# V' copied out of PSUM in full-width rows, and laid out by DMAs within SBUF

## The chip, the cores and the metric

One NeuronCore of a Trainium2 chip runs the kernel. TensorE (PE) multiplies and transposes, VectorE (DVE) and ScalarE (ACT) read PSUM and work element by element, GpSimd (POOL) works on SBUF, and SyncE (SP) issues the DMAs. The metric is the device time of one execution in microseconds (us); lower is better.

## The reference

Cross-attention and a quantized feed-forward network (FFN), for 128 sequences of 64 tokens with 128 features, in fp32. The attention has 16 heads of 64; the mask is causal. The FFN's weights are ternary and its activations are rounded to 8 bits.

```python
x = x + attention(layernorm(x), ctx, ctx, Wq, Wk, Wv, Wo, bo, mask)   # softmax(q k^T / 8) v, 16 heads of 64
x = x + ffn(layernorm(x), w_gate, w_up, w_down)
# bitlinear(a, w) = act_quant(a) @ weight_quant(w)^T
# ffn(a) = bitlinear(silu(bitlinear(a, w_gate)) * bitlinear(a, w_up), w_down)
```

## The kernel before

**Tiling.** Two sequences make a pair of 128 tokens, one per partition. There are 64 pairs, in 16 groups of four. The projections are folded: K' = ctx (Wk Wq^T / 8) for each head, so that the scores are layernorm(x) times K', and V' = ctx (Wv Wo) for each head, so that the product of the probabilities with V' is the attention's output, summed over the heads. K' and V' need the accuracy of fp32 and are made of three matmuls each (high x high, high x low, low x high parts).

**Slots.** The work runs in 64 slots, one per pair, and three more that drain the pipeline. In slot s, TensorE computes the scores of pair s, the product of pair s - 1 (L492 to L496), and transposes and FFN matmuls of pairs s - 1 to s - 3. Between these stand four units of V' of pair s (`v_quarter`, v0 to v3, L381) and four of K' of the next group (`k_quarter`, k0 to k3, L400), each of three matmuls of 512 columns into a PSUM bank. The order by hand is: scores; in a group's first slot v0; transposes, gate and up matmuls, in the other slots v0; transposes, k0, down matmul, v1, k1, product, v2, k2, k3, v3; and after v3 of a group's fourth slot the transposes of context and x of the group after next. The last group has no K' units in its slots. Each engine runs its own list in this order and waits on semaphores; nothing else sets the order.

**Banks.** V' units go to ps_s (v1, v2) and ps_kv (v0, v3), K' units to ps_kv (k0, k3) and ps_s (k1, k2). A bank can be written again once ScalarE has copied it: K' quarter 2 waits on `k_evac` for the copy of quarter 1 (L408), and the scores, which use both ps_s banks, wait for the copies of v2 and k2, in a group's first slot also for that of k3.

**V' and its layout.** A unit of V' is made for 128 context tokens, with columns for 4 of the 8 head pairs and 128 features. u // 2 says which head of a pair it is (h2), u % 2 which half of the head pairs. The product contracts over the 64 tokens of both heads of a pair together, so that it wants `vp[h2 * 64 + token, b, head pair, feature]`, with sequence b of the pair in the free dimension. PSUM has sequence b in the partitions. `take_v` (L576) therefore makes two copies a unit, one for each sequence, each of 64 partitions x 512, from partitions b * 64 on to partitions h2 * 64 on. That is eight such copies a slot, each with a count on `v_evac`. The product waits for eight a slot.

**ScalarE's order in a slot** (L594 to L625): xq_t, hid_t, probabilities' first half, tanh, v0, probabilities' second half, k0, v1, the exponential of pair s (which waits on POOL's subtraction of the row maximum), k1, v2, k2, k3, v3, and in a group's fourth slot context and x of a later group.

**SP's order**: after the setup's loads, for each group, the loads of x and context of the group after next, the load of the residual's x for the next group, and the store of the group before.

Of the kernel before, what the change touches and what calls it, by code (L numbers as in the profile page):

```python
# [40 lines left out]
def build(nc, x, ctx, mask, wq, wk, wv, wo, bo, w_gate, w_up, w_down, ident, causal, chooser, out):  # L41
# [19 lines left out]
    with ExitStack() as es:  # L61
# [41 lines left out]
        x1 = [sb(f"x1_{i}", [P, GP, D]) for i in range(2)]  # L103

        vp = [sb(f"vp{i}", [P, 2, HP, D]) for i in range(2)]
        prob = [sb(f"prob{i}", [P, H, S]) for i in range(2)]
        prob_t = sb("prob_t", [P, HP, P])
        row_max = [sb(f"row_max{i}", [P, H]) for i in range(2)]
# [43 lines left out]
        x_loaded = [sem(f"x_loaded{i}") for i in range(2)]  # L152
        xres_loaded = [sem(f"xres_loaded{i}") for i in range(2)]
        stored = [sem(f"stored{i}") for i in range(2)]

        const_set, absum_done, mean_ready, mean_done, tern_step = (sem(n) for n in (
            "const_set", "absum_done", "mean_ready", "mean_done", "tern_step"))
# [50 lines left out]
        @block.sync  # L208
        def _(sp):
            sp.dma_start(mask_u8.rearrange("b (p j) -> b p j", j=S),  # L210
                         mask.rearrange("(p b) j -> b p j", b=2)).then_inc(mask_in, 16)
            sp.dma_start(causal_sb[:], causal).then_inc(small_in, 16)
            sp.dma_start(choose_f[:], chooser).then_inc(small_in, 16)
            sp.dma_start(id_sb[:], ident).then_inc(id_in, 16)
            for w, src in enumerate((wk, wq, wv)):
                sp.dma_start(w_raw[w], src).then_inc(wqkv_in[w], 16)
            sp.dma_start(x_in[0][:], x_g[0]).then_inc(x_loaded[0], 16)
            sp.dma_start(ctx_in[0][:], ctx_g[0]).then_inc(ctx_loaded[0], 16)
            for w, t in enumerate((w_gate, w_up)):
                sp.dma_start(f_raw[:, w, :].rearrange("p (a d) -> p a d", d=D),  # L220
                             t.rearrange("(a p) d -> p a d", p=P)).then_inc(ffn_in, 16)
            sp.dma_start(f_raw[:, 2, :], w_down).then_inc(ffn_in, 16)
            sp.dma_start(wo_sb, wo.rearrange("(a p) e -> p a e", p=P)).then_inc(wo_in, 16)
            sp.dma_start(bo_sb[:], bo.rearrange("(o d) -> o d", o=1).broadcast_to([P, D])).then_inc(bo_in, 16)
            sp.dma_start(x_in[1][:], x_g[1]).then_inc(x_loaded[1], 16)
            sp.dma_start(ctx_in[1][:], ctx_g[1]).then_inc(ctx_loaded[1], 16)
            sp.dma_start(x_res[0][:], x_g[0]).then_inc(xres_loaded[0], 16)

            def group(it, par):

                g = 2 * it + par
                dyn = lambda v, k: v[g + k] if isinstance(it, int) else v[bass.ds(g + k, 1)].rearrange(
                    "o p q d -> (o p) q d")
                if group_ahead(it, par * GP, 2):
                    sp.wait_ge(xn_ready, GP * g + GP)
                    sp.dma_start(x_in[par][:], dyn(x_g, 2)).then_inc(x_loaded[par], 16)
                    sp.wait_ge(ctxt_ready, g + 1)
                    sp.dma_start(ctx_in[par][:], dyn(ctx_g, 2)).then_inc(ctx_loaded[par], 16)
                if group_ahead(it, par * GP, 1):
                    if not isinstance(it, int) or g:  # L240
                        sp.wait_ge(x1_done, GP * g)
                    sp.dma_start(x_res[1 - par][:], dyn(x_g, 1)).then_inc(xres_loaded[1 - par], 16)
                if not isinstance(it, int) or g:
                    sp.wait_ge(x2_done, GP * g)
                    sp.dma_start(dyn(out_g, -1), x1[1 - par][:]).then_inc(stored[1 - par], 16)

            for it in range(BODIES):
                for par in range(2):
                    group(it, par)

            sp.wait_ge(x2_done, PAIRS - 1)
            sp.dma_start(out_g[GROUPS - 1][:, 0:GP - 1, :], x1[1][:, 0:GP - 1, :]).then_inc(stored[1], 16)
            sp.wait_ge(x2_done, PAIRS)
            sp.dma_start(out_g[GROUPS - 1][:, GP - 1, :], x1[1][:, GP - 1, :]).then_inc(stored[1], 16)
            sp.wait_ge(stored[0], 16 * BODIES)
            sp.wait_ge(stored[1], 16 * (BODIES + 1))
# [3 lines left out]
        def _(pe):  # L260
# [116 lines left out]
            def slot(it, c):  # L377
# [3 lines left out]
                def v_quarter(u):  # L381

                    v_dst = banks[v_bank(it, c, u)]
                    if live(it, c):
                        if first(it, c):
                            pe.wait_ge(n_lo_done, u + 1)
                        if u == 0 and live(it, c, 1):
                            pe.wait_ge(v_evac, 8 * s)
                        elif u == 1:
                            pe.wait_ge(biased, s + 1)  # L390
                        elif u and group_ahead(it, c, 1):
                            pe.wait_ge(v_evac, 8 * s + (4, 2)[u == 3])
                        h2, half = u // 2, u % 2
                        hi, lo = (w[:, h2, 4 * half:4 * half + 4, :].rearrange("p a e -> p (a e)") for w in (n_hi, n_lo))
                        cols = slice(q * P, q * P + P)
                        mm(v_dst, ct_hi[par][:, cols], hi, start=True, stop=False)  # L396
                        mm(v_dst, ct_hi[par][:, cols], lo, start=False, stop=False)  # L397
                        mm(v_dst, ct_lo[par][:, cols], hi, start=False, stop=True).then_inc(v_ready, 1)  # L398
# [12 lines left out]
                if live(it, c):  # L411
# [4 lines left out]
                    if first(it, c):  # L416
                        pe.wait_ge(mean_done, 1)
                    if live(it, c, 1):
                        pe.wait_ge(v_evac, 8 * s - 2)
                        if not isinstance(it, int) or group_ahead(it, c - 1, 1):  # L420
                            pe.wait_ge(k_evac, 16 + 4 * s - 1)
                    for half in range(2):
# [63 lines left out]
                if live(it, c, 1):  # L486

                    pe.wait_ge(pt_evac, 2 * s)
                    pe.wait_ge(v_evac, 8 * s)
                    if live(it, c, 3):  # L490
                        pe.wait_ge(x2_done, s - 2)
                    for a in range(HP):  # L492
                        for b in range(2):
                            t = mm(ps_a[b * S:(b + 1) * S, 0:D], prob_t[:, a, b * S:(b + 1) * S],  # L494
                                   vp[(c - 1) % 2][:, b, a, :], start=(a == 0), stop=(a == HP - 1))
                    t.then_inc(attn_ready, 1)  # L496
# [16 lines left out]
        def _(act):  # L513
# [58 lines left out]
            def slot(it, c):  # L572
# [3 lines left out]
                def take_v(u):  # L576
                    if live(it, c):

                        h2, half = u // 2, u % 2
                        act.wait_ge(v_ready, 4 * s + u + 1)  # L580
                        for b in range(2):
                            copy(flat(vp[c % 2][h2 * S:(h2 + 1) * S, b, 4 * half:4 * half + 4, :]),
                                 banks[v_bank(it, c, u)][b * S:(b + 1) * S, :]).then_inc(v_evac, 1)

                def take_k_quarter(u):
                    if live(it, c) and group_ahead(it, c, 1):
# [328 lines left out]
```

## Time and profile before

| | us |
|---|---|
| median of 3 timed runs | 815.12 |
| lowest, highest | 815.04, 815.55 |
| the profiled execution | 815.8 |
| its span on the core | 814.0 |
| TensorE busy in it | 783.2 (96%) |
| ScalarE busy | 678.6 (83%) |
| VectorE busy | 677.9 (83%) |
| POOL busy | 406.9 (50%) |
| DMA traffic | 20.84 MB, 26 GB/s on average |

The profile records one execution by engine; times in its rows are microseconds from the start of the span, unless ns is said. "Busy" adds up the engine's instructions. Matmuls are pipelined and their ends are modelled, so a busy TensorE is not one at its peak. The chain is followed back from the last instruction: at each step to what released it, or to the instruction before it on its engine.

### The profile page before, as it was taken

The page shows a single profiled execution, that of the slowest core. Times are in us where ns is not written, and L with a number is a line of the kernel's source. Part 1 is how long each engine was busy: PE and PEld are TensorE (multiplying, and loading weights), DVE is VectorE, ACT ScalarE, POOL GpSimd, SP SyncE. Part 2 cuts the span into 40 slices and gives each one's busy share as a digit, 9 for nine tenths or more (in the row PEclk, how much of TensorE's full clock was granted, in tenths as well). Part 3 has the DMA queues.
Part 4 walks back from the last instruction along what each step waited for, and adds up shares of the span by engine and source line. Part 5 has one row for each costly group of instructions (what it writes and reads, how often), then busy time and mean ns, then how long its engine had stood idle before and what let it go on. Part 6 is the DMA issues. An engine that isn't in the chain of part 4 may idle for free.

```text
span 814.0 us, 15482 instructions
## 1 busy us (share of the span) xinstructions
PE 783.2 (96%) x5487; PEld 543.7 (67%) x5550; DVE 677.9 (83%) x1845; ACT 678.6 (83%) x1202; POOL 406.9 (50%) x404
## 2 busy tenths in 40 slices
PE   7899999999999999999999999999999999999983
PEld 5657667666766766666676676676676667667652
DVE  7749888888888888888888888888888888878894
ACT  4688888888888888988888888888888888888872
POOL 1234545455455555555555545555455554544551
PEclk9999999999999999999999999999999999999997
DMA  7200010000101001010100101010010100000000
GB/s 219 61 1 1 15 39 16 22 18 14 41 13 40 5 17 33 14 41 14 39 1 14 41 14 40 14 40 2 13 41 14 40 14 15 0 14 14 2 14 14
DMA packets 37123, 20.84 MB, mean 26 GB/s; under 512 B 1460, under 2 KB 36534, under 8 KB 37046
## 3 DMA queue, kind: packets, MB, share of 16 engines
q1 hardware_dynamic: 37046, 19.84, 8.5%
q8 instruction: 45, 0.74, 0.4%
q14 instruction: 32, 0.26, 0.1%
HBM read 15.64 MB, written 4.19 MB: 24 GB/s over the span
## 4 chain that ended last, share of the span: by engine, by line
PE 91%; DVE 4%; ACT 2%; issue 2%; POOL 1%; DMA 0%; POOLq 0%; DVEq 0%
PE ps_s L425 14%; PE ps_a L494 14%; PE ps_s L396 5%; PE ps_s L316 4%; PE ps_kv L396 4%; PE ps_kv L397 3%; PE ps_kv L316 3%; PE ps_kv L317 3%; PE ps_s L318 3%; PE ps_s L398 3%; PE ps_s L397 3%; PE ps_b L453 3%; PE ps_s L317 3%; PE ps_kv L398 3%; PE ps_kv L318 3%; PE ps_a L453 3%
## 5 line engine op out<-in xcount | busy, mean ns | idle before, releaser
L866 POOL TENSOR_TENSOR prob<-prob,row_max 128x1024 f32<-128x1024 f32 x64 | 121.9, 1905 | 179.6 <-DVE row_max L741 179.6
L514 ACT ACTIVATE vp<-ps_s 64x512 f32<-64x512 f32 x256 | 151.2, 591 | 33.2 <-PE ps_s L398 28.9
L884 POOL TENSOR_TENSOR prob<-prob,row_rec 128x512 f32<-128x512 f32 x128 | 130.7, 1042 | 56.5 <-DVE row_rec L816 56.5
L514 ACT ACTIVATE vp<-ps_kv 64x512 f32<-64x512 f32 x256 | 151.5, 592 | 5.3
L876 POOL TENSOR_TENSOR hid_b<-hid_q,neg_round 128x512 bf16<-128x512 f32 x64 | 66.5, 1039 | 124.3 <-DVE hid_q L785 124.3
L494 PE MATMUL ps_a<-vp,prob_t 128*64 128x128 f32 x2048 | 125.9, 276 | 1.3 <-DVE x L763 1.2
L494 PEld LDWEIGHTS ps_a<-vp,prob_t 128*64 128x64 f32 x2048 | 110.6, 137 | 24.3 <-issue 16.3
L425 PE MATMUL ps_s<-kp,xn_t 128*64 128x512 f32 x512 | 124.0, 605 | 2.9 <-ACT vp L514 1.9
L738 DVE TENSOR_TENSOR prob<-ps_s,bias_sb 128x1024 f32<-128x1024 f32 x64 | 78.4, 1225 | 51.8 <-PE ps_s L425 51.7
L843 POOL TENSOR_TENSOR rs<-ve,neg_half 128x1 f32<-128x1 f32 x128 | 70.2, 548 | 42.0 <-DVE ve L663 25.0
L514 ACT ACTIVATE kp<-ps_s 128x512 f32<-128x512 f32 x130 | 77.8, 598 | 11.8 <-PE ps_s L284 8.0
L741 DVE TENSOR_REDUCE row_max<-prob 128x16 f32<-128x1024 f32 x64 | 78.1, 1220 | 2.2
L814 DVE TENSOR_REDUCE row_sum<-prob 128x16 f32<-128x1024 f32 x64 | 77.4, 1210 | 0.0
L514 ACT ACTIVATE kp<-ps_kv 128x512 f32<-128x512 f32 x122 | 72.3, 593 | 0.6 <-PE ps_kv L284 0.5
L425 PEld LDWEIGHTS ps_s<-kp,xn_t 128*64 128x64 f32 x512 | 31.0, 136 | 60.4 <-issue 55.3
L514 ACT ACTIVATE xq_t<-ps_u 128x128 bf16<-128x128 f32 x64 | 17.8, 278 | 62.7 <-PE ps_u L438 62.7
L570 ACT ACTIVATE prob<-prob 128x1024 f32<-128x1024 f32 x64 | 66.9, 1045 | 0.0
L396 PE MATMUL ps_s<-n_hi,ct_hi 128*128 128x512 f32 x128 | 62.5, 489 | 0.7 <-ACT vp L514 0.7
L396 PE MATMUL ps_kv<-n_hi,ct_hi 128*128 128x512 f32 x128 | 61.4, 480 | 0.0
L316 PE MATMUL ps_kv<-ct_hi,m_hi 128*128 128x512 f32 x120 | 52.5, 438 | 1.0 <-ACT wd_t L514 1.0
L754 DVE SCALAR_TENSOR_TENSOR gated<-tanh_sb,ps_g 128x512 f32<-128x512 f32 x64 | 43.9, 687 | 10.2 <-ACT tanh_sb L606 8.8
L316 PE MATMUL ps_s<-ct_hi,m_hi 128*128 128x512 f32 x128 | 52.0, 406 | 0.3
(175 smaller groups left out, 1734.8 us busy)
## 6 DMA issues: line engine op xcount, KB each, us to landing
x_in<-in_x SPq DMA_DIRECT2D x16, 256.0 KB, 3.9
ctx_in<-in_ctx SPq DMA_DIRECT2D x16, 256.0 KB, 4.4
x_res<-in_x SPq DMA_DIRECT2D x16, 256.0 KB, 2.8
out<-x SPq DMA_DIRECT2D x15, 256.0 KB, 2.5
kp<-in_L_xattn_Wk SPq DMA_DIRECT2D x1, 512.0 KB, 3.7
kp<-in_L_xattn_Wq SPq DMA_DIRECT2D x1, 512.0 KB, 4.6
kp<-in_L_xattn_Wv SPq DMA_DIRECT2D x1, 512.0 KB, 5.5
kp<-in_L_xattn_Wo SPq DMA_DIRECT2D x1, 512.0 KB, 6.1
```

The lines of the kernel that those rows point to most:

```text
L316: mm(dst, hi, ct_hi[par][:], start=True, stop=False)
L396: mm(v_dst, ct_hi[par][:, cols], hi, start=True, stop=False)
L425: t = mm(ps_s[b * S:(b + 1) * S, half * BANK:(half + 1) * BANK], xn_t[par][:, cols], kp[par][:, half * 8:half * 8 + 8, cols], start=True, ...
L494: t = mm(ps_a[b * S:(b + 1) * S, 0:D], prob_t[:, a, b * S:(b + 1) * S], vp[(c - 1) % 2][:, b, a, :], start=(a == 0), stop=(a == HP - 1))
L514: copy = lambda dst, src, **kw: nc.scalar.activation(dst, src, ACT.Copy, **kw)
L570: nc.scalar.activation(prob[c % 2][:], prob[c % 2][:], ACT.Exp).then_inc(exp_done, 1)
L738: v.tensor_tensor(prob[c % 2][:], ps_s[:, :].rearrange("p (h j) -> p h j", j=S), pair_bias.broadcast_to([P, H, S]), ALU.add).then_inc(bias ...
L741: v.tensor_reduce(row_max[c % 2][:], prob[c % 2][:], AX, ALU.max).then_inc(max_done, 1)
L814: v.tensor_reduce(row_sum[:], prob[c % 2][:], AX, ALU.add).then_inc(sum_step, 1)
L843: p.tensor_tensor(dst[:], src[:], neg_half[:], ALU.pow).then_inc(done, 1)
L866: p.tensor_tensor(prob[c % 2][:], prob[c % 2][:], rows(row_max[c % 2]), ALU.subtract).then_inc(shifted, 1)
L884: p.tensor_tensor(prob[c % 2][:, heads, :], prob[c % 2][:, heads, :], rows(row_rec[c % 2])[:, heads, :], ALU.mult).then_inc(normed, 1)
```

## The change

`take_v` makes one copy a unit, of all 128 partitions, into a new tile `v_rows[h2]` that has the partitions of PSUM (token within sequence b). When both units of an h2 are copied, SP issues two DMAs, one for each sequence, that bring 64 partitions x 4096 bytes from `v_rows[h2]` to `vp`. That is four DMAs a slot. They count on `v_moved[h2]`, 32 a slot. The product waits on both of these and no longer on `v_evac`; ScalarE waits on `v_moved[h2]` of the slot before when it writes `v_rows[h2]` again; and SP waits for the product of the pair before the last (`attn_ready`) before it writes `vp`. `v_evac` counts 4 a slot, with the same meaning for the banks as before. SP's list is now written slot by slot: the group's loads and stores stand between the moves. The loads of x and context, for three groups ahead, come in the third slot, that of the residual in the second, the store in the fourth.

```diff
+        v_rows = [sb(f"v_rows{i}", [P, HP, D]) for i in range(2)]
...
+        v_moved = [sem(f"v_moved{i}") for i in range(2)]
...
+            def load_inputs(g):
+                par = g % 2
+                sp.wait_ge(xn_ready, GP * (g - 2) + GP)
+                sp.dma_start(x_in[par][:], x_g[g]).then_inc(x_loaded[par], 16)
+                sp.wait_ge(ctxt_ready, g - 1)
+                sp.dma_start(ctx_in[par][:], ctx_g[g]).then_inc(ctx_loaded[par], 16)
+
+            def slot(it, c):
+                s = BODY * it + c
+                g, q, par = 2 * it + c // GP, c % GP, c // GP % 2
+                if q == 3 and g > 0 and live(it, c):
+                    sp.wait_ge(x2_done, GP * g)
+                    sp.dma_start(out_g[g - 1], x1[1 - par][:]).then_inc(stored[1 - par], 16)
+                for h2 in range(2):
+                    if live(it, c):
+                        sp.wait_ge(v_evac, 4 * s + 2 * h2 + 2)
+                        if live(it, c, 2):
+                            sp.wait_ge(attn_ready, s - 1)
+                        for b in range(2):
+                            sp.dma_start(vp[c % 2][h2 * S:(h2 + 1) * S, b, :, :],
+                                         v_rows[h2][b * S:(b + 1) * S, :, :]).then_inc(v_moved[h2], 16)
+                if q == 1 and live(it, c) and group_ahead(it, c, 1):
+                    if g:
+                        sp.wait_ge(x1_done, GP * g)
+                    sp.dma_start(x_res[1 - par][:], x_g[g + 1]).then_inc(xres_loaded[1 - par], 16)
+                if q == 2 and live(it, c) and group_ahead(it, c, 3):
+                    load_inputs(g + 3)
+
+            load_inputs(2)
+            slots(slot, 0)
...
-                    pe.wait_ge(v_evac, 8 * s)
+                    pe.wait_ge(v_moved[0], 32 * s)
+                    pe.wait_ge(v_moved[1], 32 * s)
...
                         act.wait_ge(v_ready, 4 * s + u + 1)
-                        for b in range(2):
-                            copy(flat(vp[c % 2][h2 * S:(h2 + 1) * S, b, 4 * half:4 * half + 4, :]),
-                                 banks[v_bank(it, c, u)][b * S:(b + 1) * S, :]).then_inc(v_evac, 1)
+                        if live(it, c, 1):
+                            act.wait_ge(v_moved[h2], 32 * s)
+                        copy(flat(v_rows[h2][:, 4 * half:4 * half + 4, :]), banks[v_bank(it, c, u)]).then_inc(v_evac, 1)
```

The other changed waits follow the new count of `v_evac` (8 * s becomes 4 * s, and so on).

On ScalarE, from the tanh of a slot on, before: L514 is the copy, L570 the exponential, and x2 stands for two instructions of the same kind in a row.

```order
L606 ACTIVATE tanh_sb<-ps_g,g_half 128x512
L514 ACTIVATE vp<-ps_kv 64x512 x2
L514 ACTIVATE prob_t<-ps_b 128x512
L514 ACTIVATE kp<-ps_kv 128x512
L514 ACTIVATE vp<-ps_s 64x512 x2
L570 ACTIVATE prob<-prob 128x1024
L514 ACTIVATE kp<-ps_s 128x512
L514 ACTIVATE vp<-ps_s 64x512 x2
```

The same place on ScalarE now:

```order
L619 ACTIVATE tanh_sb<-ps_g,g_half 128x512
L527 ACTIVATE v_rows<-ps_kv 128x512
L527 ACTIVATE prob_t<-ps_b 128x512
L527 ACTIVATE kp<-ps_kv 128x512
L527 ACTIVATE v_rows<-ps_s 128x512
L583 ACTIVATE prob<-prob 128x1024
L527 ACTIVATE kp<-ps_s 128x512
L527 ACTIVATE v_rows<-ps_s 128x512
```

The order is the same; each pair of half-height copies is one of full height, so that two copies fewer stand ahead of the exponential and of the K' copy behind it.

On SP, the DMAs of some groups of the steady part, before: loads of x and context, load of the residual's x, store.

```order
L236 DMA x_in<-in_x 128x4x128 [waits xn_ready]
L238 DMA ctx_in<-in_ctx 128x4x128 [waits ctxt_ready]
L242 DMA x_res<-in_x 128x4x128 [waits x1_done]
L245 DMA out<-x_0 128x4x128 [waits x2_done]
L236 DMA x_in<-in_x 128x4x128 [waits xn_ready]
```

The same on SP now, from the second slot of a group to the store in the fourth:

```order
L251 DMA vp<-v_rows 64x1024 [waits attn_ready,v_evac]
L251 DMA vp<-v_rows 64x1024
L256 DMA x_res<-in_x 128x4x128 [waits x1_done]
L251 DMA vp<-v_rows 64x1024 [waits attn_ready,v_evac]
L251 DMA vp<-v_rows 64x1024
L251 DMA vp<-v_rows 64x1024 [waits attn_ready,v_evac]
L251 DMA vp<-v_rows 64x1024
L235 DMA x_in<-in_x 128x4x128 [waits xn_ready]
L237 DMA ctx_in<-in_ctx 128x4x128 [waits ctxt_ready]
L244 DMA out<-x_0 128x4x128 [waits x2_done]
```

Two moves follow each half's copies, and the loads and the store of a group have moved in among them.

On TensorE, the product (L494 before) and what stands around it:

```order
L318 MATMUL ps_s<-ct_hi,m_lo 128x512
L494 MATMUL ps_a<-vp,prob_t 64x128 [waits x2_done,v_evac,pt_evac]
L494 MATMUL ps_a<-vp,prob_t 64x128 x15
L396 MATMUL ps_s<-n_hi,ct_hi 128x512 [waits v_evac]
L397 MATMUL ps_s<-n_lo,ct_hi 128x512
L398 MATMUL ps_s<-n_hi,ct_lo 128x512
```

And now (L507 is the product):

```order
L330 MATMUL ps_s<-ct_hi,m_lo 128x512
L507 MATMUL ps_a<-vp,prob_t 64x128 [waits v_moved1,x2_done,v_moved0,pt_evac]
L507 MATMUL ps_a<-vp,prob_t 64x128 x15
L408 MATMUL ps_s<-n_hi,ct_hi 128x512 [waits v_evac]
L409 MATMUL ps_s<-n_lo,ct_hi 128x512
L410 MATMUL ps_s<-n_hi,ct_lo 128x512
```

Nothing has changed its place on TensorE; the product waits for the moves in place of the copies.

## Rows read from the trace of the kernel before

**Rows 1.** The page: busy time (share of the span) by engine, and the last chain.

```profile
PE 783.2 (96%) x5487; PEld 543.7 (67%) x5550; DVE 677.9 (83%) x1845; ACT 678.6 (83%) x1202; POOL 406.9 (50%) x404
...
PE 91%; DVE 4%; ACT 2%; issue 2%; POOL 1%; DMA 0%; POOLq 0%; DVEq 0%
```

**Rows 2.** Groups by line and shape: out<-in, shapes, count, busy us, mean ns, idle before.

```profile
L514 ACT ACTIVATE vp<-ps_kv 64x512 f32<-64x512 f32 x256 | 151.5, 592 | 5.3
...
L514 ACT ACTIVATE kp<-ps_s 128x512 f32<-128x512 f32 x130 | 77.8, 598 | 11.8 <-PE ps_s L284 8.0
```

**Rows 3.** Busy us by engine in two stretches; last: TensorE's clock, DMA share, GB/s.

```profile
400.00:500.00 100.00, 99.53 (x715) 69.29 (x722) 85.84 (x239) 86.62 (x155) 52.95 (x54) 1.00 0.11 30
...
760.00:780.00 20.00, 18.41 (x148) 12.33 (x147) 19.02 (x50) 16.70 (x30) 11.06 (x10) 1.00 0.04 13
```

**Rows 4.** The chain in a group's first slot: start us, us, engine, tile, line.

```profile
427.63 0.02 issue
427.66 0.50 PE ps_s L316
```

**Rows 5.** Waits between 60 and 740 us: in total, times, longest.

```profile
PEld ps_s L316 <- ACT kp L514: 6.6, 15, 0.5
```

**Rows 6.** Timeline of the same slot, ScalarE and POOL: start us, us, instruction.

```profile
425.94 1.04 ACT L570 ACTIVATE prob<-prob 128x1024 f32<-128x1024 f32 x1
427.01 0.60 ACT L514 ACTIVATE kp<-ps_s 128x512 f32<-128x512 f32 x1
...
422.43 1.91 POOL L866 TENSOR_TENSOR prob<-prob,row_max 128x1024 f32<-128x1024 f32 x1 [2.40 <-DVE row_max L741]
```

**Rows 7.** The chain in slots 0 and 1.

```profile
44.34 0.60 ACT vp L514
...
47.89 0.23 PE ps_kv L398
...
53.82 1.90 PE ps_a L494 x32
```

**Rows 8.** Timeline of slot 60 on TensorE and VectorE: start us, us, instruction, idle before.

```profile
752.87 1.94 PE L425 MATMUL ps_s<-kp,xn_t 128*64 128x512 f32 x8 [0.30 <-ACT kp L514]
...
758.33 1.97 PE L494 MATMUL ps_a<-vp,prob_t 128*64 128x128 f32 x32
...
760.63 0.28 DVE L801 TENSOR_TENSOR x<-ps_a,x_res 128x128 f32<-128x128 f32 x1
```

**Rows 9.** The chain in two steady slots.

```profile
404.48 0.23 PE ps_kv L318
...
405.18 0.23 PE ps_kv L398
...
412.17 1.90 PE ps_a L494 x32
...
417.08 0.44 PE ps_b L274 x4
```

**Rows 10.** The page's DMA issues: count, KB each, median us from issue to landing.

```profile
ctx_in<-in_ctx SPq DMA_DIRECT2D x16, 256.0 KB, 4.4
x_res<-in_x SPq DMA_DIRECT2D x16, 256.0 KB, 2.8
...
kp<-in_L_xattn_Wk SPq DMA_DIRECT2D x1, 512.0 KB, 3.7
kp<-in_L_xattn_Wq SPq DMA_DIRECT2D x1, 512.0 KB, 4.6
```

**Rows 11.** Timeline of SP's issues, at the start and in one group: start us, us.

```profile
2.27 0.43 SPq L216 DMA_DIRECT2D kp<-in_L_xattn_Wk  x1
2.74 0.43 SPq L216 DMA_DIRECT2D kp<-in_L_xattn_Wq  x1
...
400.09 0.51 SPq L236 DMA_DIRECT2D x_in<-in_x  x1
400.64 0.56 SPq L238 DMA_DIRECT2D ctx_in<-in_ctx  x1
```

More of the change, by code:

```diff
@@ L227, in _ @@
             sp.dma_start(x_res[0][:], x_g[0]).then_inc(xres_loaded[0], 16)
[L229 to L240, printed above, removed]
-                        sp.wait_ge(x1_done, GP * g)
[L242 to L245, printed above, removed]
@@ L247, in _ @@
-            for it in range(BODIES):
-                for par in range(2):
-                    group(it, par)
+            def load_inputs(g):
[20 more added lines that the diff above has]
+                    if g:
+                        sp.wait_ge(x1_done, GP * g)
+                    sp.dma_start(x_res[1 - par][:], x_g[g + 1]).then_inc(xres_loaded[1 - par], 16)
+                if q == 2 and live(it, c) and group_ahead(it, c, 3):
+                    load_inputs(g + 3)
@@ L387, in v_quarter @@
                         if u == 0 and live(it, c, 1):
-                            pe.wait_ge(v_evac, 8 * s)
+                            pe.wait_ge(v_evac, 4 * s)
                         elif u == 1:
@@ L391, in v_quarter @@
                         elif u and group_ahead(it, c, 1):
-                            pe.wait_ge(v_evac, 8 * s + (4, 2)[u == 3])
+                            pe.wait_ge(v_evac, 4 * s + (2, 1)[u == 3])
                         h2, half = u // 2, u % 2
@@ L418, in slot @@
                     if live(it, c, 1):
-                        pe.wait_ge(v_evac, 8 * s - 2)
+                        pe.wait_ge(v_evac, 4 * s - 1)
                         if not isinstance(it, int) or group_ahead(it, c - 1, 1):
@@ L488, in slot @@
                     pe.wait_ge(pt_evac, 2 * s)
-                    pe.wait_ge(v_evac, 8 * s)
+                    pe.wait_ge(v_moved[0], 32 * s)
+                    pe.wait_ge(v_moved[1], 32 * s)
                     if live(it, c, 3):
```

## The prediction

> **What bounds the kernel now.** I read the page's busy times first: TensorE is busy for 783.2 of 814.0 us, VectorE and ScalarE for 678 each, and the chain of work that ended last lies on TensorE for 91% and on ScalarE for 2% [rows 1]. So ScalarE's 151.5 us of copies of V' out of ps_kv, and as much again out of ps_s [rows 2], are no price by themselves. The question is where TensorE waits for ScalarE. The table by stretch says how much room there is: in 400 to 500 us TensorE is busy for 99.53 of 100 us at the full granted clock [rows 3]. But a busy row hides short waits, since matmuls are pipelined, so I read the chain in order of time and looked for pieces longer than their like. Between 50 and 750 us every kind of piece has one price wherever it stands (a matmul of 512 columns that follows its like 0.23 or 0.24 us, the product 1.90), with one exception: in the first slot of groups 1 to 14, the first matmul of K' quarter 2 takes 0.50 us after 0.02 of issue [rows 4]. The wait is for ScalarE: the weight loads of that line sat for 6.6 us in 15 times until a copy of K' ended [rows 5], which is 0.46 in each of these 14 slots and 0.18 in an early one that TensorE does not feel. In that slot ScalarE has also taken the next group's context and x out of PSUM, and is late from there on: v0, v1 (two copies each), the exponential from 425.94, then the K' copy that ends at 427.61 [rows 6].
>
> Two more places: at the start, the second of two copies of V' in a row stands in the chain with 0.60 us [rows 7]; and near the end the scores of slot 60 begin at 752.87 after 0.30 us of waiting for a copy of K' [rows 8]. From there VectorE takes over: from 760 to 780 us it is busy for 19.02 of 20, TensorE for 18.41 and ScalarE for 16.70 [rows 3]. TensorE's waits for ScalarE in slots 61 to 63 therefore cost nothing.
>
> **What is removed: four of eight copies a slot.** A copy of 64 partitions x 512 takes 592 ns; one of 128 x 512 out of the same kind of bank (a K' copy) 598 [rows 2]. The time goes by columns, so each pair becomes one of 0.59: ScalarE loses 4 x 0.59 = 2.4 us a slot, 151 us in all. On the path this gives:
> - First slots of groups 1 to 14. Since v0 and v1 take one copy each, ScalarE reaches the exponential 1.2 us earlier, at about 424.8 instead of 425.94; POOL's subtraction, its input, ends at 424.34 [rows 6], so the full 1.2 can be had up to 0.4. Then the copy of K' quarter 1 ends at about 426.4, and the weight load that wants it could begin 0.46 before 427.66, at 427.2. The piece falls from 0.02 + 0.50 to 0.23: 0.29 us each, **14 x 0.29 = 4.1 us**.
> - Start: one of two copies in the chain goes: **0.6 us**.
> - Slot 60: the copy ahead of the two K' copies is 0.6 shorter, so the 0.30 wait goes: **0.3 us**. VectorE's pace from there on stays.
> - All other slots: nothing. The chain is TensorE work there, and less work on ScalarE moves none of it.
>
> **What is added: the moves.** Four a slot, each 64 partitions x 4096 bytes = 256 KB, 64 MB in all, on SP's queue. Three things have to be seen.
>
> First, who waits. The product of pair s in slot s + 1 now waits for both halves. The half that counts is the second, since v3 is the last unit of slot s; the first half is issued half a slot earlier, with some 12 us to spare. ScalarE waits for a half before it writes v_rows again: v0 of the next slot for moves issued some 8 us earlier, and v2 for moves that the product ahead of it has waited for already; nothing there.
>
> Second, the budget. In a steady slot the last matmul of v3 ends at 405.18 + 0.23 = 405.41 and the product begins at 412.17 [rows 9], its first weight load some 0.1 earlier. v3's copy, no longer behind the pair of v2, runs from 405.43 to 406.03, so from SP's first issue to the landing of the second move there are **6.0 us**. In first slots of a group the transposes of context and x, two pieces of 0.44 [rows 9], lengthen it to 6.9. In slot 1, without the FFN's work, v3's last matmul ends at 47.89 + 0.23, its copy 0.61 later, and the product begins at 53.82: 5.0 with the 0.1 of the weight load [rows 7]. In slot 60 the scores, which follow v3, begin at 752.57 without the wait, and the product at 758.33 - 0.30; that makes 4.9, and 0.3 more since VectorE takes the product's result only at 760.63, 0.3 after its end [rows 8].
>
> Third, the landing. No row shows a DMA from SBUF to SBUF, nor one of 64 partitions. Lower bound: the 256 KB loads of x_res land 2.8 us after issue [rows 10]; with a second issued 0.43 later that is 3.2 us. Nearest in form are the weight loads at the start, with the same 4096 bytes a partition, 512 KB each: two issued at 2.27 and 2.74 us land after 3.7 and 4.6 [rows 10, 11], that is 1.37 us apart, and 3.7 - 1.37 = 2.3 us is fixed. At this full rate a 256 KB move drains in 0.69 and the second lands after 2.3 + 2 x 0.69 = 3.7. Half the partitions may carry no more than half the rate, and I take that: 2.3 + 2 x 1.37 = **5.1 us**. A pair of loads from DRAM, x_in and ctx_in, gives nearly this by another way: issued at 400.09 and 400.64, 0.55 + 4.4 = 4.95 [rows 10, 11]. Upper bound: reading and writing the same memory halve the rate again, 2.3 + 2 x 2.74 = 7.8 us. I take 5.1, since two different rows come close to it: under the budget of 6.0 by 0.9, so hidden; over that of slot 1 by about **0.2 us**, which I count as a loss; in slot 60 covered by VectorE's 0.3.
>
> The Trainium skill, in "SBUF — State Buffer", section "Door 1: The DMA port swizzle", has a rule that speaks against moves of this shape: partitions 0 to 63 (or 64 to 127) reach only 8 of 16 DMA ports, 196 GB/s measured at 1 MiB; and its section "Can I just issue two DMAs to hit both halves?" says that two such transfers run one after the other. By its figures two moves would take about 2 + 2 x 1.3 = 4.6 us, an estimate from that page; with full rate on its 16 ports it would be 3.2. Either is under 6.0 and leaves the sum as it is. No run here shows it yet.
>
> SP's queue: four issues of 0.43 [rows 11] are 1.7 us of a slot of some 12. The loads and the store of a group now stand between moves, at places where what they wait for was done a slot earlier; the x_in and ctx_in loads go behind the second half of the third slot, and the next move is half a slot away. Before this they were waited for nowhere; x_in is loaded one slot or more ahead of its first reader. Nothing.
>
> **Sum.** 4.1 + 0.6 + 0.3 - 0.2 = 4.8 us. The profiled execution took 815.8 us with a span of 814.0; the median of the timed runs is 815.12. I expect a span of about 809.2 and a median of 815.1 - 4.8 = **810.3 us**.
>
> **Rivals.**
> - *The moves land late.* The distance from v3's copy to the product becomes longer than the TensorE work between, and TensorE stands before the product in every slot. At the upper bound of 7.8: 44 steady slots x 1.8 + 14 first slots x 0.9 + 2.8 in slot 1 + 4 last ones x 2.6 = 105 us, less 5.0 gained: 915 us. The point from which it decides is low: 4.8 us lie in 44 x 0.11, so the kernel is slower from a landing at 6.1 us. For it: no row shows such a transfer. Against it: the DMA engines have a share of only 0.11 here [rows 3], and both near rows say 5. Chance 0.18.
> - *The 14 stalls stay*, because the exponential waits for POOL's subtraction or for something in front of it that I see only from outside. Then 0.6 + 0.3 - 0.2 = 0.7 is left: 814.4 us. Against it: 0.4 us of room at the exponential and 0.8 at the K' copy. Chance 0.09.
> - *The moves' traffic slows the engines a little*, or a few slots are late by a tenth. The moves drain for some 5.5 of 12 us; 0.08 us lost per slot takes all of the gain: 815 us. Against it: while the 512 KB of loads issued at 400.09 and 400.64 were under way, a matmul at 404.48 kept its 0.23 [rows 9, 11]. Chance 0.08.
>
> **How the numbers follow.** My forecast has 0.65, with 809 to 812 of its own. A measurement of this kernel can tell about 0.2%, 1.6 us. The second and third rival lie within that: 0.17. Faster 0.65, same 0.17, slower 0.18. The range reaches from 808.8 (slot 1 not late, and a little more at the end) over both middle cases and the mildest of the late ones, a landing at up to 6.1 or 6.2, to 818; what is left out is most of the first rival.
>
> **What would show it.** ScalarE about 527 us busy. In the chain, K' quarter 2's first matmul at 0.23 in all first slots. The product's matmuls preceded by no wait for a DMA except in slot 1. DMA share near 0.4 to 0.5 in the steady stretch, moves landing 3 to 4.5 us after their issue. What makes it wrong: waits for a DMA at the product in steady slots, so that more than 6.76 us lie between the end of v3 and the product (405.41 to 412.17 [rows 9]).

## The result and the profile after

| | before | after |
|---|---|---|
| median of 5 timed runs, us | 815.55 | 811.62 |
| lowest, highest | 815.04, 816.84 | 811.16, 812.50 |
| the profiled execution | 815.8 | 811.4 |
| its span | 814.0 | 809.6 |

The ratio is 0.9953 with an interval of 0.9938 to 0.9967: faster by half a percent, clear of the noise, by 3.9 us in the medians and 4.4 in the spans. The forecast was a gain of 4.8 us.

The page of the kernel after, its busy times, chain and DMA issues (to be held against [rows 1, 10]):

```profile
PE 783.0 (97%) x5550; PEld 544.5 (67%) x5550; DVE 678.4 (84%) x1845; ACT 532.9 (66%) x946; POOL 407.4 (50%) x404
...
PE 89%; DVE 6%; issue 1%; DMA 1%; ACT 1%; POOL 1%; POOLq 0%; SPq 0%; DVEq 0%
...
vp<-v_rows SPq DMA_DIRECT2D x256, 256.0 KB, 3.7
```

ScalarE is busy for 532.9 us in place of 678.6, and TensorE for the same 783: 146 us of work gone, 4 us of time. The copies, by line and shape, have half their count at the same price (592 ns before [rows 2]):

```profile
L527 ACT ACTIVATE v_rows<-ps_kv 128x512 f32<-128x512 f32 x128 | 76.7, 599 | 6.7
```

The stretch of [rows 3], 400 to 500 us, in the same columns:

```profile
400.00:500.00 100.00, 100.00 (x700) 68.58 (x699) 85.76 (x240) 67.36 (x120) 54.31 (x54) 1.00 0.45 109
```

TensorE has no idle time left in it (99.53 before), and the DMA engines have a share of 0.45 where they had 0.11. The chain in the same slot as [rows 4]; L328 is the line that was L316:

```profile
422.29 1.90 PE ps_a L507 x32
424.18 0.43 PE ps_s L408
424.62 0.23 PE ps_s L409
424.85 0.24 PE ps_s L410
425.09 0.23 PE ps_s L328
```

The piece of 0.50 with 0.02 of issue before it is now one of 0.23. The timeline of ScalarE and POOL shows why [rows 6]:

```profile
419.87 1.91 POOL L879 TENSOR_TENSOR prob<-prob,row_max 128x1024 f32<-128x1024 f32 x1 [2.41 <-DVE row_max L754]
...
421.63 0.60 ACT L527 ACTIVATE v_rows<-ps_s 128x512 f32<-128x512 f32 x1
422.12 1.05 ACT L583 ACTIVATE prob<-prob 128x1024 f32<-128x1024 f32 x1
423.07 0.59 ACT L527 ACTIVATE kp<-ps_s 128x512 f32<-128x512 f32 x1
```

The subtraction ends at 421.78, the exponential follows at 422.12, and the K' copy is done at 423.66, 1.4 us before the matmul at 425.09 that needs its bank. In the trace of before that copy ended at 427.61, for a matmul at 427.66.

**One product is late.** In the whole trace the product waits for a DMA once (0.4 us in all, 1 time, 0.4 the longest):

```profile
PE ps_a L507 <- DMA vp<-v_rows: 0.4, 1, 0.4
```

The chain there:

```profile
545.92 0.61 ACT v_rows L527
...
546.54 0.46 SPq L251
547.00 0.04 issue
547.04 5.73 DMA vp<-v_rows
552.78 0.25 issue
553.02 1.97 PE ps_a L507 x32
```

And SP's issues behind that move (start us, us):

```profile
547.69 0.62 SPq L235 DMA_DIRECT2D x_in<-in_x  x1
548.36 1.51 SPq L237 DMA_DIRECT2D ctx_in<-in_ctx  x1
549.91 1.15 SPq L244 DMA_DIRECT2D out<-x  x1
```

This second move landed 5.73 us after its issue. It is the slowest of the 256, whose minimum, median and maximum are:

```profile
DMA to landing us min/median/max: 2.9/3.7/5.7
```

The pair before it in the same place of its group, issued at 498.87, took 3.3 and 3.9, so its second landed some 4.4 us after the first issue. So the loads and the store behind it do not by themselves do this.

Another row of the trace goes with the long landings. Besides SP's transfers the DMA engines carry two queues that the profile calls `instruction`; by that name they bring the program's own instructions. While the late pair was under way, from 546.5 to 552.8 us, a packet of each ran (queue: packets, MB, share of the 16 engines):

```profile
q8 instruction: 1, 0.02, 0.9%
q14 instruction: 1, 0.01, 0.3%
```

From 498.8 to 503.4 us, with the pair that has the same loads behind it, there was none. And in slot 16 (237.1 to 242.6 us), where SP issues no load or store between this pair and the next, the second move landed 5.4 us after the first issue, with one such packet under way:

```profile
q8 instruction: 1, 0.02, 1.1%
```

Over the whole trace, no pair without an `instruction` packet in flight has its second landing later than 4.64 us after its first issue, and each of the four slowest pairs of the second half (slots 9, 16, 29 and 42, 5.4 to 6.2 us) has a q8 packet in flight. Three further traces that have one late product (ScalarE's rounding and the two with added matmuls, below) show the same, with 4.60 to 4.64 as the limit. Not every such packet goes with a long landing: some pairs with one under way land after 4.2 to 4.4. So the `instruction` packets are the first suspect; no experiment moved them, so this stays a coincidence in the rows and not a shown cause.

**The end.** In the last slot TensorE stands idle for long stretches, and then runs at a granted clock of 0.55 of 2.4 GHz on average (800 is near the end of the span; columns as in [rows 3]):

```profile
798.00:802.00 4.00, 2.28 (x11) 1.16 (x11) 1.85 (x6) 1.52 (x3) 0.00 (x0) 0.55 0.00 0
```

The kernel before does the same: its clock is 0.60 in 802 to 804 us and 0.50 from there on.

### The profile page after: what moved, and what is told of

Its sections match the earlier page's. It is cut to its first block, busy times and chain, and to the rows that moved or that the text cites. A ratio compares the mean times of both kernels' runs of the same rounds, so it can differ in the third digit from the quotient of the medians.

```text
span 809.6 us, 15983 instructions
## 1 busy us (share of the span) xinstructions
PE 783.0 (97%) x5550; PEld 544.5 (67%) x5550; DVE 678.4 (84%) x1845; ACT 532.9 (66%) x946; POOL 407.4 (50%) x404
## 4 chain that ended last, share of the span: by engine, by line
PE 89%; DVE 6%; issue 1%; DMA 1%; ACT 1%; POOL 1%; POOLq 0%; SPq 0%; DVEq 0%
PE ps_s L437 14%; PE ps_a L507 14%; PE ps_s L408 5%; PE ps_kv L408 4%; PE ps_s L330 3%; PE ps_kv L328 3%; PE ps_s L328 3%; PE ps_kv L329 3%; PE ps_s L329 3%; PE ps_kv L409 3%; PE ps_s L410 3%; PE ps_s L409 3%; PE ps_kv L410 3%; PE ps_kv L330 3%; PE ps_b L465 3%; PE ps_a L465 3%
## 5 line engine op out<-in xcount | busy, mean ns | idle before, releaser
L527 ACT ACTIVATE v_rows<-ps_s 128x512 f32<-128x512 f32 x128 | 76.7, 599 | 106.8 <-PE ps_s L410 106.5
L507 PE MATMUL ps_a<-vp,prob_t 128*64 128x128 f32 x2048 | 125.9, 276 | 1.6 <-DVE x L776 1.2
L507 PEld LDWEIGHTS ps_a<-vp,prob_t 128*64 128x64 f32 x2048 | 110.6, 137 | 24.7 <-issue 21.8
L527 ACT ACTIVATE v_rows<-ps_kv 128x512 f32<-128x512 f32 x128 | 76.7, 599 | 6.7
L408 PE MATMUL ps_s<-n_hi,ct_hi 128*128 128x512 f32 x128 | 62.5, 489 | 0.1
L408 PE MATMUL ps_kv<-n_hi,ct_hi 128*128 128x512 f32 x128 | 61.4, 480 | 0.0
L328 PE MATMUL ps_kv<-ct_hi,m_hi 128*128 128x512 f32 x120 | 52.6, 438 | 1.0 <-ACT wd_t L527 1.0
L409 PE MATMUL ps_kv<-n_lo,ct_hi 128*128 128x512 f32 x128 | 51.0, 398 | 0.0
```

The costliest lines, as they stand in the source:

```text
L328: mm(dst, hi, ct_hi[par][:], start=True, stop=False)
L527: copy = lambda dst, src, **kw: nc.scalar.activation(dst, src, ACT.Copy, **kw)
```

## The experiments

All are held against runs of the kernel before on the same chip in the same session; its median was 815.85 for the half-height copies without counts, the other order, and the one or two more moves; 815.83 for the moves over 128 partitions and ScalarE's rounding alone; 815.54 for the others.

### Where the gain comes from

**Half-height copies again, with the moves kept.** An edit of the kernel after:

```diff
-copy(flat(v_rows[h2][:, 4 * half:4 * half + 4, :]), banks[v_bank(it, c, u)]).then_inc(v_evac, 1)
+for b in range(2):
+    rows = slice(b * S, b * S + S)
+    t = copy(flat(v_rows[h2][rows, 4 * half:4 * half + 4, :]), banks[v_bank(it, c, u)][rows, :])
+t.then_inc(v_evac, 1)
```

> The changed kernel with its four moves a slot, but each unit of V' copied in two half-height copies again, now into v_rows. If the gain comes from the shorter work of ScalarE alone, ScalarE's busy time is back at about 680 us, the 14 stalls before K' quarter 2 stand again in first slots (0.50 instead of 0.23 us), the second copy stands in the chain of slot 0, and the time is that of before, about 815.5 us. If the moves, or the new order of SP's loads, brought it, the time stays at 811.6.

Measured: 818.34 us (817.57 to 819.71), ratio 1.0035, interval 1.0022 to 1.0047. All of the gain is gone, so it came from the copies; and 2.5 us more are lost than the kernel before has. The first slots lose 0.35 us each in place of 0.25 (from one down matmul to the next 12.02 us, where it is 11.67 in the kernel after and 11.92 in the one before); that is 1.4. The rest is at four products that wait for a move (1.4 us in all) and in the last slots. The last of the four (product, start us, us, idle before):

```profile
791.07 1.97 PE L507 MATMUL ps_a<-vp,prob_t 128*64 128x128 f32 x32 [0.58 <-DMA vp<-v_rows]
```

With eight copies a slot the last one of v3 ends at least one copy (0.6) later, and the budget of the moves shrinks by that. The profiled execution is the slowest of the five (819.71), and 0.66 us of its longer span lie ahead of slot 0, where the kernels do the same work: the first scores begin at 34.02 us there. In the other traces, of both kernels and of the other experiments, they begin between 32.32 and 33.77 us, so a few tenths of any difference between two spans are of this kind.

**The same with a count on each copy**, as the kernel before has it, so that SP, TensorE and the copies wait on counts of 8 a slot. It asks whether the 0.10 more per first slot comes from the pair's first copy having no count of its own.

```diff
-sp.wait_ge(v_evac, 4 * s + 2 * h2 + 2)
+sp.wait_ge(v_evac, 8 * s + 4 * h2 + 4)
...
-copy(flat(v_rows[h2][:, 4 * half:4 * half + 4, :]), banks[v_bank(it, c, u)]).then_inc(v_evac, 1)
+for b in range(2):
+    rows = slice(b * S, b * S + S)
+    copy(flat(v_rows[h2][rows, 4 * half:4 * half + 4, :]),
+         banks[v_bank(it, c, u)][rows, :]).then_inc(v_evac, 1)
```

> The changed kernel with half-height copies again, as in the first experiment, but each copy counts for itself, as in the kernel before, and not the second for both. The first came out 2.8 us over the kernel before where I expected nothing: 1.4 of it were stalls before K' quarter 2 of 0.35 instead of 0.25 us. If that tenth comes from the missing count between two copies and not from the moves, it goes: about 816.9 us, with stalls of 0.25. If the moves cause it, they stay at 0.35 and the time at 818.3. The rest, products of the last slots that wait for a move, stays by either.

Measured: 818.55 us (818.26 to 819.64), ratio 1.0039, interval 1.0025 to 1.0052. The missing count is not the cause: first slots take 12.07, a stall of 0.40. By the expectation that points to the moves, but how they would do it is not seen in the chain of such a slot:

```profile
426.18 0.59 ACT v_rows L527
426.77 0.03 issue
426.80 1.06 ACT prob L583
427.86 0.02 issue
427.88 0.61 ACT kp L527
428.49 0.04 issue
428.53 0.50 PE ps_s L328
```

Here the exponential begins 0.03 after the end of the copy before it, while in the kernel before it began 0.09 before that end (copy pair until 426.03, exponential at 425.94). Why these instructions overlap less is open: the copies differ in their target and in ScalarE's wait for the last moves, and no run separated the two. In the last slots the chain is now a ring: copies, SP's issue, the move, the product, copies. Two of its moves, the first two rows with the product behind each:

```profile
776.06 3.73 DMA vp<-v_rows
...
780.04 1.97 PE ps_a L507 x32
...
785.91 4.08 DMA vp<-v_rows
...
790.24 1.97 PE ps_a L507 x32
```

**The kernel before with another order and no DMA.** If the first slots' stall is all that the copies cost, then ScalarE can have it back by making the K' copy ahead of the exponential in those slots:

```diff
+k_first = q == 0 and s > 0
+if k_first:
+    take_k_quarter(1)
 if live(it, c) and not first(it, c):
     exponential(s, c)
-take_k_quarter(1)
+if not k_first:
+    take_k_quarter(1)
```

> The kernel before, without any move, with one thing exchanged on ScalarE: in the first slot of groups 1 to 14 the copy of K' quarter 1 stands ahead of the exponential. If the stall of TensorE before quarter 2 is all that the change gains in the steady part, these 14 stalls of 0.25 us go and the time is 815.5 - 3.6 = about 812 us, with ScalarE as busy as before. If the stall was only a mark in the records and the gain has another source, it stays at 815.5.

Measured: 811.72 us (811.41 to 812.55), ratio 0.9954, interval 0.9942 to 0.9967. That is the median of the change, with ScalarE busy for 678.2 us and not one move. First slots take 11.67, so the stall itself is worth 3.55 us over the 14 of them. That the medians agree to 0.1 us is partly luck. In the spans this order gains 4.1: the 3.55, and 0.8 ahead of slot 0, where it changes nothing (scores at 32.56 us, at 33.36 before), less some tenths at the end. The start and slot 60, which the change shortens by 0.9, are as long here as before. In the timeline of ScalarE the K' copy of that slot now stands ahead of the exponential, and TensorE's piece is one of 0.23:

```profile
423.46 0.60 ACT L514 ACTIVATE kp<-ps_s 128x512 f32<-128x512 f32 x1
423.95 1.05 ACT L570 ACTIVATE prob<-prob 128x1024 f32<-128x1024 f32 x1
```

### How much room the moves have

**One more move a slot** of 256 KB from v_rows into a spare tile, ahead of the second half's two and counted with them:

```diff
+if h2 == 1:
+    for n in range(1):
+        sp.dma_start(v_spare[n][S:2 * S, :, :], v_rows[1][n * S:(n + 1) * S, :, :]).then_inc(v_moved[1], 16)
 for b in range(2):
     sp.dma_start(vp[c % 2][h2 * S:(h2 + 1) * S, b, :, :],
...
-pe.wait_ge(v_moved[1], 32 * s)
+pe.wait_ge(v_moved[1], 48 * s)
```

> The changed kernel with one more move of 256 KB, to a spare tile, ahead of the two of the second half in each slot. In the changed kernel the second move lands some 4.4 us after the first issue, 1.1 after the other. With three the last lands after about 5.5. If the budget is 6.0 us in steady slots, they stay at 11.67; slot 1 (budget 5.0) and the last four (4.9 to 5.2) lose 1 to 2 us together: 812 to 814 us. If the margin is smaller than I think, by x us, it is 44 x more.

Measured: 817.97 us (816.36 to 820.25), ratio 1.0029, interval 1.0018 to 1.0041. In most steady slots nothing is lost (slots of 11.67 as before): the last of three moves lands 5.5 to 5.7 us after the first issue, just inside the budget. But ten products are late, and the waits of the whole trace are:

```profile
PE ps_a L511 <- DMA vp<-v_rows: 7.5, 10, 2.0
```

Six of them stand where the budget is small: slot 1 with 0.63, and the last five products of all. The other four (0.18 to 0.95 us) are single ones in the steady part. The last of all:

```profile
798.89 2.92 PE L511 MATMUL ps_a<-vp,prob_t 128*64 128x128 f32 x32 [2.04 <-DMA vp<-v_rows]
```

The expectation priced the last slots far too low.

**Two more moves a slot**, the same edit with `range(2)` and 64 for 48.

> The same with two more moves. The last lands after about 6.6 us, which is over the budget of 6.0 by 0.6 in 44 steady slots (26 us), under that of 6.9 in 14 first slots, over by 1.6 in slot 1 and by about 1.4 in each of the last four: 811.6 + 26 + 1.6 + 5.6 = about 845 us, with waits for a DMA before the product in the steady slots. If the budget is right but late moves are absorbed elsewhere, it is under 820.

Measured: 885.85 us (883.87 to 886.37), ratio 1.0856, interval 1.0841 to 1.0871. The waits of the whole trace, and one steady slot, first the product and then its chain from the first issue on:

```profile
PE ps_a L511 <- DMA vp<-v_rows: 67.1, 51, 2.7
```
```profile
419.61 1.97 PE L511 MATMUL ps_a<-vp,prob_t 128*64 128x128 f32 x32 [1.09 <-DMA vp<-v_rows]
```
```profile
412.43 0.46 SPq L253
...
414.25 5.02 DMA vp<-v_rows
419.27 0.34 issue
```

The product in the slot behind a group's first (at 406.81) waits for nothing, the other three of that group for 1.0 to 1.1 each; elsewhere single ones wait for up to 2.7. The last of four moves lands 6.84 us after the first issue (412.43 to 419.27), and the product begins 0.34 later. Without the wait it would have begun at 418.52, so what the landing may take is about 5.8 us and not 6.0. A first slot, which has 0.9 us more, just about holds 6.84. The expectation took 6.6 and 6.0, a wait of 0.6 where 1.0 to 1.1 came; that, the last slots and the single late ones are what it was short by. The first rival of the prediction was right in its mechanism, and its price is steep: two moves too many turn a gain of 4 us into a loss of 70.

**The same bytes over 128 partitions.** Each move takes all partitions and half of the columns:

```diff
-sp.dma_start(vp[c % 2][h2 * S:(h2 + 1) * S, b, :, :],
-             v_rows[h2][b * S:(b + 1) * S, :, :]).then_inc(v_moved[h2], 16)
+heads = slice(4 * b, 4 * b + 4)
+sp.dma_start(vp[c % 2][:, h2, heads, :], v_rows[h2][:, heads, :]).then_inc(v_moved[h2], 16)
```

> The changed kernel with moves of the same 256 KB, the same number and the same places in SP's list, but each over 128 partitions x 2048 bytes instead of 64 x 4096. It leaves the layout out: V' stays in the partitions it has in PSUM, so the output is another. If 64 partitions halve the rate, the second move of a pair lands earlier than 4.4 us after the first issue, by about 0.9: 3.5. If a transfer within SBUF has its rate whatever the partitions, it is 4.4 again. The time is 811.6 by either, since both are under the budget; the late single move of the profile (5.7 us) may be gone, 0.4 us less.

Measured: 811.31 us (810.51 to 812.22), ratio 0.9944, interval 0.9930 to 0.9957. The time hardly differs from that of the kernel after; the moves do:

```profile
vp<-v_rows SPq DMA_DIRECT2D x256, 256.0 KB, 2.5
```
```profile
400.00:500.00 100.00, 100.00 (x701) 68.61 (x700) 85.66 (x240) 67.35 (x120) 54.21 (x54) 1.00 0.31 109
```

They land 2.5 us after their issue where those of 64 partitions took 3.7, and the DMA engines are busy for 0.31 in place of 0.45, for the same 109 GB/s. The second of a pair lands 3.0 us after the first issue, where 3.5 was expected. No product waits for a move in this trace. The Trainium skill says in "SBUF — State Buffer", section "Door 1: The DMA port swizzle", that a transfer of partitions 0 to 63 or 64 to 127 reaches half of the ports; these two rows agree. The bytes per partition were halved together with it, and no run separates the two.

**The second half in four pieces of 128 KB**, two of them issued after v2:

```diff
-for h2 in range(2):
+for h2, heads, done in ((0, slice(0, 8), 2), (1, slice(0, 4), 3), (1, slice(4, 8), 4)):
...
-        sp.wait_ge(v_evac, 4 * s + 2 * h2 + 2)
+        sp.wait_ge(v_evac, 4 * s + done)
```

> The changed kernel with the second half's two moves cut in two by columns: 128 KB each, the first two issued already when v2 is copied, the last two after v3. If drain time is what stands between v3's copy and the landing, the last lands some 3.6 us after the issue that follows v3, instead of 4.4, and the one late product of the profile is gone: 811.2 us, the same within what can be told. If two more issues a slot (some 1 us of SP) or twice the number of moves get in the way, it is over 812.

Measured: 811.39 us (810.57 to 812.71), ratio 0.9950, interval 0.9936 to 0.9964. The 128 KB moves land after 2.3 us, the last of them 2.9 us after the issue that follows v3 (3.6 was expected), and no product waits for one:

```profile
vp<-v_rows SPq DMA_DIRECT2D x256, 128.0 KB, 2.3
```

The span is 808.8, against 809.6 with the one late product. In the medians, 811.39 and 811.62, the difference is too small to be told.

### The end of the kernel

**ScalarE takes a step of VectorE's in slots 60 to 63.** From slot 60 on VectorE sets the pace [rows 3], and ScalarE now has time. It makes the rounding of the hidden activations (hid_q, 0.5 us of VectorE a slot) there:

```diff
+if act_rounds(s):
+    act.wait_ge(h_step, H_STEPS * (s - 2) + 6)
+    copy(hid_q[:], hid[:], scale=qs3[:], bias=ROUND).then_inc(hq_ready, 1)
...
-v.tensor_scalar(hid_q[:], hid[:], qs3[:], ROUND, ALU.mult, ALU.add).then_inc(hq_ready, 1)
+if not act_rounds(s):
+    v.tensor_scalar(hid_q[:], hid[:], qs3[:], ROUND, ALU.mult, ALU.add).then_inc(hq_ready, 1)
```

> The changed kernel, with the rounding of the hidden layer (0.49 us on VectorE) done by ScalarE in slots 60 to 63, where it has the time now. If VectorE alone sets the pace of the last four slots (9.65 us), each becomes some 0.45 us shorter: about 809.9 us. If ScalarE's or TensorE's chain is close behind, little of it is seen: 811 or more.

Measured: 811.16 us (810.95 to 812.14), ratio 0.9946, interval 0.9932 to 0.9959. The slots become 9.59, 9.47 and 9.46 us long, from 9.78, 9.64 and 9.63: 0.17 to 0.19 each and not 0.45, since VectorE, with less to do, now waits for the product:

```profile
775.08 0.29 DVE L825 TENSOR_TENSOR x<-ps_a,x_res 128x128 f32<-128x128 f32 x1 [0.27 <-PE ps_a L510]
```

And the next slot takes 10.21 in place of 9.22, which gives it all back; the one behind it is shorter again, 8.24 in place of 8.83, so that 0.14 us are left from the down matmul of slot 61 to the last. The windows show what the long slot goes with:

```profile
786.00:788.00 2.00, 0.00 (x0) 0.00 (x0) 1.86 (x7) 0.60 (x1) 1.55 (x3) 1.00 0.36 104
788.00:790.00 2.00, 1.56 (x10) 1.47 (x11) 0.48 (x3) 0.88 (x2) 1.22 (x2) 0.51 0.90 229
```

After more than 2 us without a matmul TensorE comes back at a granted clock of 0.51, the level of 1.2 GHz, and a row of four transposes takes 0.87 us where it takes 0.44 at 2.4 GHz:

```profile
789.32 0.87 PE ps_a L468 x4
```

**Matmuls that nobody reads, in the last three slots.** They keep TensorE at work while it waits, alone and with the edit before. 8, 14 and 22 matmuls of 512 columns are added:

```diff
+keep_busy(s, (8, 14, 0)[s - PAIRS] if s >= PAIRS else 0)
...
+keep_busy(s, 22 if s == PAIRS + 2 else 0)
...
+def keep_busy(s, n):
+    if n:
+        pe.wait_ge(v_evac, 4 * PAIRS)
+    for _ in range(n):
+        mm(ps_s[:, 0:BANK], ct_hi[1][:, 0:P], n_hi[:, 0, 0:4, :].rearrange("p a e -> p (a e)"),
+           start=True, stop=True)
```

> The changed kernel with the same added matmuls after slot 63 and nothing else. In its profile the clock fell only after slot 64: the pieces of TensorE from 798 us on would be shorter by 0.15 + 0.22 + 0.2 + 0.2 = 0.8 us: 810.8. By the rival, 811.6 or more.

Measured alone: 810.15 us (810.03 to 811.20), ratio 0.9934, interval 0.9921 to 0.9948.

> The sixth experiment (ScalarE rounds in slots 60 to 63) with added matmuls on TensorE in its idle times after slot 63 (8, 14 and 22 of 512 columns, into a bank that nobody reads). There the granted clock fell to about half before slot 64's transposes, and what four slots had gained (0.5 us) was given back. If the clock of the tail is what it costs, the pieces there are as short as elsewhere (0.22 instead of 0.44 us for four transposes) and some 1.6 us go: 809.5 us. If the added matmuls only stand in the way, or the clock falls all the same, 811 or more.

Measured with ScalarE's rounding: **809.73 us** (809.00 to 810.69), ratio 0.9930, interval 0.9917 to 0.9942. It is the fastest median of all kernels here. The same windows in this kernel, and the one near the end:

```profile
788.00:790.00 2.00, 2.00 (x18) 1.47 (x16) 0.18 (x1) 1.35 (x4) 0.92 (x1) 1.00 0.75 197
...
798.00:802.00 4.00, 4.00 (x20) 2.98 (x21) 2.76 (x7) 1.07 (x2) 0.00 (x0) 1.00 0.16 49
```

The clock is 1.00 in both. The tail's slots are 9.46, 9.05 and 8.40 us long where the edit before had 9.46, 10.21 and 8.24. Against the kernel after, from the down matmul of slot 61 to the last (752.92 to 806.52 us there), the added matmuls alone save 0.43 us in the trace, while the medians differ by 1.5. The profiled execution of the added matmuls alone is its slowest (811.20, the others 810.03 to 810.62), its first scores begin 0.44 us later than in the kernel after, and it has the same late product, so the traces compare a slow one with a fast one. How much of the 1.5 is the clock is open; with ScalarE's rounding, the same stretch is 0.99 shorter with the added matmuls than without them. The intervals of these kernels and of the kernel after overlap, so that the order among them is less sure than that each beats the kernel before.

## Why the prediction was right, and where it was off

The forecast was 810.3 us, 4.8 less than the kernel before; 811.62 came, 3.9 less in the medians and 4.4 in the spans. Point by point, in the spans:

- **The first slots** were to give 14 x 0.29 = 4.1. From one product to the next the slot went from 11.92 to 11.66 or 11.67, 3.55 over the 14. The mechanism was right, and the half-height copies (back to a stall) and the other order (no stall without a move) both show it. The term was mis-sized by 0.03 to 0.04 each: the chain's pieces of 0.02 and 0.50 were held against one of 0.23, but the pieces around it give some of that back. The distance between two products would have been the better row.
- **The start** gave the 0.6 expected: TensorE's chain there has no copy in it (44.18 0.09 issue, then L408 at 44.27), where [rows 7] had one of 0.60, and from the scores of slot 0 to those of slot 1 it is 14.08 us in place of 14.70. **Slot 60** gave 0.3. Behind it VectorE's pace was to stay; between the products of slots 61 and 62 it is 9.63 us for 9.76.
- **Slot 1** was to be late by 0.2 and was not. The term behind it was the landing: 5.1 us from SP's first issue to the second landing was taken, 4.4 came. That 64 partitions drain more slowly was right (3.7 us to land, against 2.5 over 128), but the landings of a pair lie only 1.1 us apart for 256 KB, while 1.37 was taken, from loads of twice the bytes [rows 10, 11]. Two of these leave some 2.2 fixed where 2.3 was taken. What failed was the step 2.3 + 2 x 1.37, which let half the partitions halve the rate of a 512 KB load from DRAM. The estimate from the Trainium skill's page "SBUF — State Buffer", 4.6, was closer.
- **The budget** of 6.0 left 0.1 between landing and product for the first weight load; the chain has 0.25 there (552.78), and 0.34 with four moves. It is nearer 5.8. The 4.9 for slot 60 is 4.8 by the prediction's own way, since the weight load's 0.1 was not taken off. Neither changed the sum.
- **The one late product** at 553.02, 0.4 us, was not in the sum. The step that failed was "Nothing" for what else is on the DMA engines: the prediction looked at what moves wait for in SP's list, and took one landing for all. Six of the 128 pairs landed more than 5.3 us after their first issue, and each of them had an `instruction` packet in flight. Loads behind the moves cost less: the second half's pairs land after 4.45 us at the median in the slots that have a load behind them (the second and third of a group) and after 4.25 in the others. The late pair had both. With the second half in pieces that finish earlier, and with moves over 128 partitions, no product was late.
- Sum in the span: 3.55 + 0.6 + 0.3 + 0.1 - 0.4 = 4.15, and 0.2 lies ahead of slot 0, where the first scores begin at 33.15 and began at 33.36. That makes 4.35 of the 4.4 measured. The 0.2 is no merit of the change, since that start differs by more between executions. That 4.8 came so near is in part luck: a loss of 0.2 that did not come stood against one of 0.4 that nobody had counted.
- **The first rival**, moves that land late, did not come, but its point of decision is real: three moves land in 5.5 to 5.7 us and are hidden in steady slots, four land in 6.84 and are late by 1.0 to 1.1. Its chance of 0.18 was fair for a transfer of which the trace had no row. **The second**, a stall that stays because of POOL, is refuted by the timeline: the exponential began 0.34 us after the subtraction's end. **The third**, that the traffic slows the engines, is refuted by 100.00 us of TensorE in 100, with slots of 11.67, at a DMA share of 0.45.
- ScalarE was to be busy for 527 us; it is 532.9.

## What to carry to other kernels

Time taken off an engine that is not the bound is worth only the places where it stands in the chain: 146 us less ScalarE work gave 4 us, and a few lines that put one copy ahead of an exponential gave 3.55 us by the trace and the same median. Look for those places first, and ask whether an order would do. A transfer put into a pipeline needs its budget (from the last instruction that makes its data to the first that reads it) worked out for every kind of slot, the first and the last ones too, and room for the spread of the landings and not for their median: look at everything that the DMA engines carry, the `instruction` queues too.

## What the runs showed of the hardware

- A move of 256 KB within SBUF over 64 partitions lands 3.7 us after its issue at the median, 2.9 at least and 5.7 at most; over 128 partitions 2.5; of 128 KB over 64 partitions 2.3.
- A pair of such moves (64 partitions, 256 KB each) has its second landing at most 4.64 us after the first issue when no `instruction` packet is in flight; the six pairs above 5.3 us all had one (kernel after).
- Between the landing of a move and the first matmul that waits for it lie 0.25 to 0.34 us.
- SP takes 0.46 us at least and 0.50 at the median to issue a move, up to 1.8 for single ones. With two more moves a slot the median of the four that were there before rises to 0.62.
- A copy out of PSUM costs 592 ns for 64 partitions x 512 and 599 for 128 x 512.
- After 2.5 us without a matmul TensorE's granted clock was 0.51 in the window from 788 to 790 us, and short transposes took twice their time (0.87 us for 0.44); with added matmuls in the idle stretches it was 1.00 in the windows of the tail in which TensorE still worked.
